# The first two attention steps are set among the layers' last three items

## The chip, the core and the metric

The kernel runs on one core of one Trainium2 chip, in one launch. The metric is the device time of that launch in microseconds (us). TensorE (PE) multiplies, VectorE (DVE), ScalarE (ACT) and GpSimd (POOL) do the rest, SyncE (SP) starts transfers; every engine works through its own list in order, and semaphores tie the lists together.

## The reference

A small language model tower: token embedding, four gated state-space layers, one attention block and one quantised linear map. Cut to what matters:

```
x = embedding[tokens] + pos                     # 32 sequences x 256 tokens x 192
for l in range(4):                              # "the layers"
    h = layernorm(x) * g + b
    u, v = split(h @ Win.T + b_in)
    uc = causal_conv4(u)
    decay = exp(-softplus(uc @ wd.T + bd)); B = uc @ wB.T; C = uc @ wC.T
    y = sum(scan(h = h * decay + uc * B) * C) * sigmoid(v)
    x = x + y @ wo.T + bo
h = layernorm(x)                                # "attention", 12 heads of 16
q, k, v = h @ wq.T, h @ wk.T, h @ wv.T ; rope on q, k
x = x + softmax(q k / 4) v @ wo.T + bo
x = x + int8_matmul(round(layernorm(x) / 0.02), weight) * 0.0002 + bias
```

## The kernel before

All 8192 rows of x (192 wide) stay in on-chip memory. The layers work on **items** of 4 tiles of 128 rows, that is two sequences: 16 items for each of 4 layers, numbered 0 to 63. The attention part works on **sequences**, 0 to 31. Both are software pipelines that are written out by hand: in each step an engine does a stage of one item, another stage of the item before, and so on. `steps` calls `step(at, l, k)` of each engine for the layers, `at(lag)` being the item that entered `lag` steps ago; after the last item has entered there are steps with `l == L` that only drain the pipeline, and k counts them from 0. `steps2` does the same for attention: `step2(at)`, with `at(None)` the number m of the step.

The names that matter here, with item 63 the last one:

- On PE: `z_c` and `b_c` (products for decay, B and C), `transposes`, and `rows`, the output product of an item, which needs the scan's result (`hc_step`, by DVE) for its second half and ends with `o_done`. For attention `turn_x1` transposes the normalised rows, `project_qk(it, t)` (t = 0, 1) and `project_v` multiply them by the weights, `turn_heads(it, g)` (g = 0 to 5) transposes the prepared q and k, and `scores` multiplies them.
- On DVE: `recurrence` (the scan of an item, from inp_h to hc_l), `save_y` and `residual` (x is updated, `x_updated`), and for attention `norm_statistics`, `norm_variances`, `norm_rows`, `save_qk`, `save_v`, `maxima`.
- On POOL: `inverse_deviation2(m)` (seven tiny operations for 1/sqrt), the rotation of q and k, the low parts of q and k (`parts`), and at the seam of the two stages six memsets of constants.
- On ACT: `turned` (a transposed tile to memory), high parts of q and k (`high_parts`), the conversion of the last weights.

Before, the order at the seam is strict: the layers drain in four steps, POOL waits for all items before its memsets, and DVE waits for those, for all items and for ACT's conversion before the first statistics:

```
            pool.wait_ge(x_updated, ITEMS)
            pool.wait_ge(s_w2, W2_ALL)
            nc.gpsimd.memset(parts[:, :, :, :, :, AUG:HS].bitcast(F32), 0.0).then_inc(s_const, 1)
...
            dve.wait_ge(s_const, 7)
            dve.wait_ge(s_w2, W2_ALL)
            dve.wait_ge(x_updated, ITEMS)
```

PSUM has eight banks. The layers use all eight; attention uses the same eight under other names (`B_W` for transposes and projections, `B_S` for scores, `B_ST` for transposed scores, `B_OT` for the outputs).

Of the kernel before, what the change touches and what calls it, by code (L numbers as in the profile page):

```python
# [47 lines left out]
def build(nc, tokens, embedding, pos_enc, w_uv_d, w_z_d, w_o_d, gain_d, vec_d, bout, w_qkv_d, b_qkv_d, w_out_d,  # L48
# [9 lines left out]
    with ExitStack() as ctx:  # L58
# [33 lines left out]
        emb = sb("emb", [P, FIRST, CT * D])  # L92

        layers_memory = ctx.enter_context(ExitStack())
# [10 lines left out]
        w_uv_rest = sa("w_uv_rest", [P, 2, 2, UV_COLS], F32R)  # L105
        w_z = sa("w_z", [P, 2, 2, Z_COLS], F32R)
        w_z_rest = sa("w_z_rest", [P, 2, 2, Z_COLS], F32R)
        w_o = sa("w_o", [P, L, 2, D])
# [6 lines left out]
        xs = sa("xs", [P, CT, 2 * D], F32R)  # L115
        ht = [sa(f"ht_{k}", [P, 2 * S], F32R) for k in range(3)]

# [5 lines left out]
        ucr_h = sa("ucr_h", [P, 2, 2 * S], F32R)  # L123

        ucr_l = sa("ucr_l", [P, 2, 2 * S], F32R)
        ucr_r = sa("ucr_r", [P, 2, 2 * S], F32R)
# [13 lines left out]
        layers_memory.close()  # L140

        qk_rows = sb("qk_rows", [P, 2, 2, 2 * D])
        parts = sb("parts", [P, 2, 2, 2, H, HS], F32R)
        q_t = sb("q_t", [P, 2, H // 2, S], F32R)
        k_t = sb("k_t", [P, 2, H // 2, S], F32R)
        v_rows = sb("v_rows", [P, 2, 2, D])
        v_aug = sb("v_aug", [P, 2, 2, H, 2 * DH])
        probs = sb("probs", [P, 2, 2, 4 * S])
        mx = sb("mx", [P, 2, 2, H])
        mx_t = sb("mx_t", [H, 2, S], F32R)  # L150
        rot = sb("rot", [P, 2, 2 * H, 2, R])
        xn1 = sb("xn1", [P, 2, 2, D])
        h1_t = sb("h1_t", [P, 2 * S])
        o_t = sb("o_t", [P, 3 * S])
        o_sum = sb("o_sum", [P, 2, H])
# [5 lines left out]
        st2 = sb("st2", [P, 4, 6])  # L161
        mv2 = sb("mv2", [P, 4, 2])
        lnt2 = sb("lnt2", [P, 3, 4])
        rstd2 = sb("rstd2", [P, 4])
# [63 lines left out]
        s_const = sem("s_const")  # L228
        mt_placed = [sem(f"mt_placed{k}") for k in range(2)]
# [16 lines left out]
        def steps(eng, step):  # L246
# [16 lines left out]
            for m in range(ITEMS, ITEMS + 4):  # L263
                step(lambda lag, m=m: item(m - lag), L, m - ITEMS)
# [37 lines left out]
        B_S, B_ST, B_OT, B_OT2 = (B_UH, B_VH), (B_UVL, B_ZH), B_BH, B_BL  # L302

        B_W = (B_ZCL, B_CH)
# [59 lines left out]
        def _(pool):  # L364
# [68 lines left out]
            inverse_deviation(item(0))  # L433

            def step(at, l, k):

                for lag, stage in ((-4, index), (-3, gather)):
                    it = at(lag)
                    if it is not None and it[1] == 0 and (l > 0 or k is None or k - lag >= FIRST):
                        stage(it[0], it[2], it[3])  # L440
                inverse_deviation(at(-1))
                bias_rows(at(0))

            steps(pool, step)


            pool.wait_ge(x_updated, ITEMS)
            pool.wait_ge(s_w2, W2_ALL)
            nc.gpsimd.memset(parts[:, :, :, :, :, AUG:HS].bitcast(F32), 0.0).then_inc(s_const, 1)
            nc.gpsimd.memset(v_aug[:, :, :, :, DH:2 * DH], 0.0).then_inc(s_const, 1)  # L450
            pool.wait_ge(s_const, 2)
            for s in range(2):
                nc.gpsimd.memset(parts[:, s, :, 1, :, AUG:AUG + 1].bitcast(F32), 1.0).then_inc(s_const, 1)
                nc.gpsimd.memset(v_aug[:, s, :, :, DH:DH + 1], 1.0).then_inc(s_const, 1)
# [26 lines left out]

            def step2(at):
# [12 lines left out]
                if it is not None:  # L495
                    n, s = it
                    for t in range(2):

                        wait(pool, qk_saved, 2 * n + t + 1)
                        wait(pool, roped, 4 * n + 2 * t)  # L500
                        w = qk_rows[:, s, t].rearrange("p (h i d) -> p h i d", i=2, d=DH // 2)[:, :, :, 0:R]
                        for i in range(2):
                            nc.gpsimd.tensor_tensor(rot[:, 0, :, i, :], w[:, :, 1 - i, :],
                                                    rope[:, 1, t, i, :][:, None, :].broadcast_to([P, 2 * H, R]), ALU.mult)
                        nc.gpsimd.tensor_tensor(rot[:, 1], w,
                                                rope[:, 0, t][:, None, :, :].broadcast_to([P, 2 * H, 2, R]),
                                                ALU.mult).then_inc(roped, 1)
                        wait(pool, roped, 4 * n + 2 * t + 1)
                        nc.gpsimd.tensor_tensor(w, rot[:, 0], rot[:, 1], ALU.add).then_inc(roped, 1)
                    for t in range(2):  # L510

                        wait(pool, hi_ready, 2 * n + t + 1)
# [20 lines left out]
        def _(pe):  # L533
# [138 lines left out]

            means(0)

            def step(at, l, k):
                uv(at(2), prepared(l, k, PREP_CENTRE))
                z_c(at(3))
                transposes(at(1))
# [215 lines left out]
        def _(act):  # L894
# [117 lines left out]
            def step(at, l, k):  # L1012
# [9 lines left out]
                if (to := prepared(l, k, PREP_ROUND)) is not None:  # L1022
                    round_weights(to)
# [521 lines left out]
```

## Time and profile before

| | us |
|---|---|
| median of 3 runs | 1673.48 (1672.98 to 1676.82) |
| the profiled execution, its own time | 1670.43 |
| its span, first to last instruction | 1668.2 |
| PE busy | 1556.8 (93%) |
| DVE busy | 1362.7 (82%) |
| ACT busy | 1241.7 (74%) |
| POOL busy | 741.5 (44%) |

The span is what the trace shows; the 2.2 us between it and the execution's own time lie before the first and after the last instruction. Times of day below are us from the span's start. PE is the busiest engine, but its share is an average over a long stage of layers (to about 988), a seam, and attention (from about 1012 on).

### The profile page before, as it was taken

How to read it: one execution, taken by the hardware profiler on the slowest of the kernel's cores; microseconds unless marked ns; L12 is line 12 of the kernel's file. 1: busy time of each engine (PE TensorE's matmuls, PEld its weight loads, DVE VectorE, ACT ScalarE, POOL GpSimd, SP SyncE). 2: the span in 40 equal slices, each digit the busy share in tenths (PEclk: the TensorE clock that was granted, in tenths of full speed). 3: DMA queues.
4: the chain of work that ended last, by engine and by line, in shares of the span. 5: the costliest groups of instructions: out<-in, count | busy, mean ns of one | idle time of the engine just before them, and what ended most of it. 6: DMA issues, size and time to landing. Idle time of an engine off the chain costs nothing.

```text
span 1668.2 us, 36353 instructions
## 1 busy us (share of the span) xinstructions
PE 1556.8 (93%) x11137; PEld 1223.6 (73%) x11137; DVE 1362.7 (82%) x3414; ACT 1241.7 (74%) x2875; POOL 741.5 (44%) x1354
## 2 busy tenths in 40 slices
PE   3699999999999999999999978999999999999985
PEld 2578788878888788888888864666666666666653
DVE  4699999899999799999999855678888887888864
ACT  2677788788888788888888833777777777777763
POOL 7655633223333233333333115556556555555542
PEclk9789999999999999999999987999999999999997
DMA  7121100000000000000000000000000000000000
GB/s 169 28 56 29 24 6 1 1 33 0 0 1 1 1 1 0 0 1 1 1 0 0 1 0 1 2 7 12 11 10 10 15 10 10 10 10 10 15 12 25
DMA packets 16397, 21.98 MB, mean 13 GB/s; under 512 B 2928, under 2 KB 13808, under 8 KB 16304
## 3 DMA queue, kind: packets, MB, share of 16 engines
q1 hardware_dynamic: 13232, 14.54, 2.7%
q0 software_dynamic: 3072, 6.30, 2.3%
q8 instruction: 47, 0.77, 0.2%
q14 instruction: 46, 0.38, 0.1%
HBM read 14.14 MB, written 6.29 MB: 12 GB/s over the span
## 4 chain that ended last, share of the span: by engine, by line
PE 76%; ACT 9%; DVE 6%; issue 6%; POOL 2%; DMA 1%; DVEq 0%; ACTq 0%; POOLq 0%
PE bank L569 14%; PE bank L560 11%; PE bank L764 5%; PE bank L721 4%; PE bank L650 4%; PE bank L735 4%; PE bank L748 4%; PE bank L580 3%; PE bank L707 3%; PE bank L700 3%; PE bank L710 3%; PE bank L621 3%; PE bank L701 3%; PE bank L657 3%; PE bank L654 2%
## 5 line engine op out<-in xcount | busy, mean ns | idle before, releaser
L1046 ACT ACTIVATE probs<-bank 128x512 f32<-128x512 f32 x384 | 207.1, 592 | 131.3 <-PE bank L748 128.5
L1376 DVE TENSOR_REDUCE mx<-bank 128x2 f32<-128x512 f32 x384 | 246.1, 682 | 22.7 <-PE bank L735 21.5
L430 POOL TENSOR_TENSOR x<-x,bo_row 128x768 f32<-128x768 f32 (+1 forms) x64 | 118.2, 1847 | 196.1 <-DVE ucr_r L1244 196.1
L560 PE MATMUL bank<-ht,w_uv 128*128 128x512 f32 x576 | 171.3, 407 | 16.7 <-ACT sv_l L1005 12.3
L748 PE MATMUL bank<-q_t,k_t 64*128 64x256 f32 x768 | 156.2, 350 | 8.5 <-ACT probs L1046 5.5
L406 POOL TENSOR_TENSOR lnt<-mv,const 128x4 f32<-128x4 f32 x64 | 20.4, 320 | 311.6 <-DVE mv L1209 311.5
L1235 DVE SCALAR_TENSOR_TENSOR uc_h<-u_h,vec,uc_h 128x512 f32<-128x512 f32 x192 | 143.2, 746 | 3.5 <-ACT uc_h L943 3.5
L560 PEld LDWEIGHTS bank<-ht,w_uv 128*128 128x128 f32 x576 | 109.2, 193 | 48.5 <-issue 17.5
L1218 DVE SCALAR_TENSOR_TENSOR xs<-x,rstd,xs 128x192 fp32r<-128x192 f32 x256 | 90.0, 414 | 65.9 <-ACT xs L982 65.9
L735 PE MATMUL bank<-k_t,q_t 64*128 64x256 f32 x768 | 135.9, 316 | 6.1 <-DVE mx L1376 2.6
L748 PEld LDWEIGHTS bank<-q_t,k_t 64*128 64x128 f32 x768 | 102.3, 186 | 39.1 <-issue 20.1
L922 ACT ACTIVATE u_l<-bank,vec 64x256 f32<-64x256 f32 x128 | 60.1, 469 | 85.5 <-PE bank L560 84.7
L560 PE MATMUL bank<-ht,w_uv_rest 128*128 128x512 f32 x384 | 123.0, 402 | 0.0
L514 POOL TENSOR_TENSOR parts<-qk_rows,parts 128x192 fp32r<-128x192 f32 x128 | 77.1, 623 | 95.9 <-ACT parts L1067 95.8
L939 ACT ACTIVATE uc_l<-bank,vec 64x256 f32<-64x256 f32 x128 | 71.9, 562 | 56.8 <-DVE inp_l L1261 55.8
L569 PE MATMUL bank<-ucr_h,w_z 128*128 128x512 f32 x256 | 108.8, 425 | 4.9 <-ACT ht L972 4.9
L721 PE MATMUL bank<-identr,parts 128*128 128x128 f32 x768 | 104.4, 260 | 4.8 <-issue 3.4
L735 PEld LDWEIGHTS bank<-k_t,q_t 64*128 64x128 f32 x768 | 95.6, 188 | 14.5 <-ACT k_t L1057 8.9
L972 ACT ACTIVATE ht<-bank 128x512 fp32r<-128x512 f32 x192 | 100.8, 597 | 4.8 <-PE bank L621 3.3
L764 PE MATMUL bank<-probs,v_aug 128*32 128x256 f32 x1536 | 103.5, 387 | 0.2 <-issue 0.2
L982 ACT ACTIVATE xs<-x,rstd 128x192 fp32r<-128x192 f32 (+1 forms) x256 | 95.6, 444 | 9.7 <-POOL rstd L418 8.1
L569 PE MATMUL bank<-ucr_r,w_z 128*128 128x512 f32 x256 | 102.0, 398 | 0.0
(178 smaller groups left out, 4618.1 us busy)
## 6 DMA issues: line engine op xcount, KB each, us to landing
out_dram<-y_out SPq DMA_DIRECT2D x32, 192.0 KB, 2.0
raw_z<-w_z_dram SPq DMA_DIRECT2D x4, 704.0 KB, 5.3
raw_uv<-w_uv_dram SPq DMA_DIRECT2D x4, 576.0 KB, 3.9
emb<-embedding_dram,idx POOLq DMA_INDIRECT x64, 3.6
q_t<-mx_t SPq DMA_DIRECT2D x64, 6.0 KB
w_o<-w_o_dram SPq DMA_DIRECT2D x1, 768.0 KB, 5.3
bo_row<-bout_dram SPq DMA_DIRECT2D x4, 96.0 KB, 6.0
w_qkv<-w_qkv_dram SPq DMA_DIRECT2D x1, 288.0 KB, 6.6
```

The lines of the kernel that those rows point to most:

```text
L430: nc.gpsimd.tensor_tensor(rows, rows, bo_row[:, l, :][:, None, :].broadcast_to([P, CT, D]), ALU.add).then_inc(x_biased, 1)
L560: last = nc.tensor.matmul(out[:], w, r[:], start=(k == 0), stop=(k == len(passes) - 1))
L569: last = nc.tensor.matmul(out[:], w, r[:, b, :], start=(k == 0), stop=(k == len(passes) - 1))
L721: last = nc.tensor.transpose(B_HEADS[g][:, (2 * o + t) * P:(2 * o + t + 1) * P].bitcast(F32R), parts[:, s, t, o, 2 * g:2 * g + 2, :].rearr ...
L735: last = nc.tensor.matmul(B_S[j][:, t * S:(t + 1) * S], q_t[q, s, g, t * P:(t + 1) * P], k_t[q, s, g, :], start=True, stop=True)
L748: last = nc.tensor.matmul(B_ST[j][:, t * S:(t + 1) * S], k_t[q, s, g, t * P:(t + 1) * P], q_t[q, s, g, :], start=True, stop=True)
L764: last = nc.tensor.matmul(bank[32 * h:32 * h + 32, c:c + S], v_aug[:, s, t, 4 * p + h, :], probs[:, (s + p) % 2, h // 2, (2 * (h % 2) + t) ...
L972: last = act.activation(ht[g][:], B_T[g][:], ACT.Identity)
L982: last = act.activation(xs[:, k, 0:D], x[:, tile_of(c, k)], ACT.Identity, scale=rstd[:, s, k:k + 1])
L1046: last = act.activation(probs[:, (s + g // 2) % 2, g % 2, 2 * j * S:2 * (j + 1) * S], B_ST[j][:], ACT.Exp, scale=float(DH) ** -0.5)
L1235: nc.vector.scalar_tensor_tensor(out=uc, in0=uk, scalar=v(l, part, V_W0 + k), in1=uc, op0=ALU.mult, op1=ALU.add).then_inc(taps, 1)
L1376: last = nc.vector.tensor_reduce(mx[:, s, :, j * H // 2 + g], B_S[j][:].rearrange("p (t k) -> p t k", t=2), AX, ALU.max)
```

## The change

The first two steps of `steps2` (m = 0 and 1: the norms of sequences 0 and 1, and q, k and v of sequence 0) no longer stand behind the layers. Each engine does its part of them inside the layers' drain steps `l == L`, k = 0, 1, 2. There are three such steps now; of the fourth, `rows(63)` on PE and `recurrence(63)`, `save_y(63)`, `residual(63)` on DVE have moved into attention's step m = 2. POOL's memsets wait only until the last product that reads the memory under them is done. So that early steps find free memory and free banks, the attention banks are renamed and the buffers stand in another order; no buffer changes its size.

```diff
-            for m in range(ITEMS, ITEMS + 4):
+            for m in range(ITEMS, ITEMS + 3):
                 step(lambda lag, m=m: item(m - lag), L, m - ITEMS)
...
+        EARLY = 2
...
-            for m in range(LEAD2):
+            for m in range(EARLY, LEAD2):
...
-        B_S, B_ST, B_OT, B_OT2 = (B_UH, B_VH), (B_UVL, B_ZH), B_BH, B_BL
-        B_W = (B_ZCL, B_CH)
+        B_W, B_S, B_ST, B_OT, B_OT2 = (B_VH, B_UVL), (B_BH, B_BL), (B_UH, B_ZH), B_ZCL, B_CH
...
POOL
-            pool.wait_ge(x_updated, ITEMS)
+            def attention_constants():
+                pool.wait_ge(uh_done, ITEMS)
...
+                if l == L and k == 0:
+                    inverse_deviation2(0)
+                    pool.wait_ge(s_w2, W2_ALL)
+                elif l == L and k == 1:
+                    pool.wait_ge(xn1_ready, 1)
+                    add_rows(0, b_out, x1_biased)
+                    inverse_deviation2(1)
+                    attention_constants()
+                elif l == L and k == 2:
+                    rotate(seq(0))
+                    pool.wait_ge(xn1_ready, 2)
+                    add_rows(1, b_out, x1_biased)
...
PE
+            def step(at, l, k):
+                first = l == L and k == 2
+                uv(at(2), prepared(l, k, PREP_CENTRE))
+                z_c(at(3))
+                transposes(at(1))
+                if first:
+                    pe.wait_ge(s_w2, W2_ALL)
+                    pe.wait_ge(sv_ready, ITEMS)
+                    turn_x1(seq(0))
+                rows(at(4))
+                if first:
+                    project_qk(seq(0), 0)
+                b_c(at(3))
+                if first:
+                    project_qk(seq(0), 1)
+                    pe.wait_ge(qk_saved, 1)
+                    project_v(seq(0))
+                    pe.wait_ge(qk_saved, 2)
+                    turn_x1(seq(1))
...
             def step2(at):
+                early = isinstance(at(None), int) and at(None) == EARLY
+                if early:
+                    rows(item(ITEMS - 1))
+                    pe.wait_ge(v_saved, 1)
+                    pe.wait_ge(inp_step, 2 * ITEMS)
...
ACT
+                if l == L and k == 0:
+                    act.wait_ge(s_w2, W2_ALL)
...
+                elif l == L and k == 2:
+                    save_h1(seq(0))
+                    act.wait_ge(s_const, 6)
+                    high_parts(seq(0), 0)
+                    high_parts(seq(0), 1)
...
DVE
+            def norm_early(m):
+                dve.wait_ge(x_updated, ITEMS - NCH + 1)
+                dve.wait_ge(var2_ready, m + 1)
+                norm_statistics(seq(m), None)
+                dve.wait_ge(stats2_done, m + 1)
+                wait(dve, rstd2_ready, m)
+                wait(dve, xn1_ready, m)
+                norm_variances(seq(m), None)
...
                 statistics_there(at(-1))
+                if early and k == 0:
+                    nc.vector.memset(mv2[:], 1.0).then_inc(var2_ready, 1)
+                elif early and k == 1:
+                    norm_rows(0, seq(0), 0, xn1[:, 0], xn1_ready)
+                elif early:
+                    norm_rows(1, seq(1), 0, xn1[:, 1], xn1_ready)
...
                 residual(at(4))
+                if early and k < 2:
+                    norm_early(k)
+                elif early:
+                    dve.wait_ge(s_w2, W2_ALL)
+                    save_qk(seq(0), 0)
+                    save_qk(seq(0), 1)
+                    save_v(seq(0))
...
             def step2(at):
+                early = isinstance(m, int) and m == EARLY
+                if early:
+                    recurrence(item(ITEMS - 1))
+                    dve.wait_ge(x_updated, ITEMS - 1)
...
                 save_qk(at(1), 0)
+                if early:
+                    save_y(item(ITEMS - 1))
+                    residual(item(ITEMS - 1))
...
                 normalise(at(5), 0)
                 maxima(at(2), 1)
```

First place, PE at the seam. Before, from `rows(63)` (L650 to L660) through `turn_x1(0)` (L693, L695), `project_qk(0, 0)` and `(0, 1)` (L700, L701), `project_v(0)` (L707, L710), to the first `turn_heads` (L721), `turn_x1(1)` and the first `scores` (L735):

```order
L650 MATMUL bank<-w_o,sv_h 128x192 x4
L654 MATMUL bank<-ones,hc_h 128x1 x4
L657 MATMUL bank<-w_o,sv_l 128x192 x4
L660 MATMUL bank<-ones,hc_l 128x1 x4
L693 MATMUL bank<-ident,xn 128x128 x2
L695 MATMUL bank<-ident,xn 64x128 x2
...
L707 MATMUL bank<-w_qkv,h_t 128x192 x2
L710 MATMUL bank<-w_qkv,h_t 128x192 x2
L721 MATMUL bank<-identr,parts 128x128 x4
L693 MATMUL bank<-ident,xn 128x128 x2
L695 MATMUL bank<-ident,xn 64x128 x2
L735 MATMUL bank<-k_t,q_t 128x256 x4
```

Of the change, the same functions in new lines: behind the last of `b_c(63)` (L595) come `project_qk(0, 1)` (L711, L712), `project_v(0)` (L718, L721), `turn_x1(1)` (L704, L706), then `rows(63)` (L676 to L686), `turn_heads` (L732) and `scores` (L746):

```order
L595 MATMUL bank<-ucr_l,w_z_rest 128x512
L711 MATMUL bank<-w_qkv,h_t 128x384
L712 MATMUL bank<-w_qkv,h_t 128x384
L718 MATMUL bank<-w_qkv,h_t 128x192 x2
L721 MATMUL bank<-w_qkv,h_t 128x192 x2
L704 MATMUL bank<-ident,xn 128x128 x2
L706 MATMUL bank<-ident,xn 64x128 x2
L676 MATMUL bank<-w_o,sv_h 128x192 x4
...
L686 MATMUL bank<-ones,hc_l 128x1 x4
L732 MATMUL bank<-identr,parts 128x128 x4
L746 MATMUL bank<-k_t,q_t 128x256 x4
```

Everything that stood between `rows(63)` and the first `turn_heads` now stands ahead of `rows(63)`; `turn_x1(1)` has left its place behind the first `turn_heads`. (`turn_x1(0)` stands further up, ahead of `rows(62)`, and `project_qk(0, 0)` between `rows(62)` and `b_c(63)`.)

Second place, DVE. Before, `save_y(62)` and `residual(62)` (L1288, L1299), then `recurrence(63)` (L1258 to L1280), then `save_y(63)` and `residual(63)`:

```order
L1288 COPY ysb<-bank 128x2 x2
L1299 SCALAR_TENSOR_TENSOR x<-bank,ysb,x 128x192 x4
L1258 SCALAR_TENSOR_TENSOR inp_h<-bank,vec,uc_h 128x512
...
L1280 TENSOR_TENSOR hc_l<-cb_l,hs_l 128x256
L1288 COPY ysb<-bank 128x2 x2
L1299 SCALAR_TENSOR_TENSOR x<-bank,ysb,x 128x192 x4
L1343 MEMSET mv 128x8
```

Of the change, from `residual(62)` (L1360) on: `save_qk(0, 0)` and `(0, 1)` (L1416), `save_v(0)` (L1425), then `recurrence(63)` (L1319 to L1341):

```order
L1360 SCALAR_TENSOR_TENSOR x<-bank,ysb,x 128x192 x4
L1416 TENSOR_TENSOR qk_rows<-bank,b_qkv 128x384 x2
L1425 COPY v_rows<-bank 128x384
L1319 SCALAR_TENSOR_TENSOR inp_h<-bank,vec,uc_h 128x512
...
L1341 TENSOR_TENSOR hc_l<-cb_l,hs_l 128x256
L1379 BN_STATS st<-x 128x6 x2
L1406 TENSOR_REDUCE mx<-bank 128x2 x2
L1386 BN_AGGR mv<-st 128x2 x2
L1416 TENSOR_TENSOR qk_rows<-bank,b_qkv 128x384
L1349 COPY ysb<-bank 128x2 x2
L1360 SCALAR_TENSOR_TENSOR x<-bank,ysb,x 128x192 x4
L1406 TENSOR_REDUCE mx<-bank 128x2 x2
```

`recurrence(63)` has moved behind three reads of PE's projections, and `residual(63)` between the first and the second pair of maxima (L1406). Beyond the seam the four engines' lists are the same as before but for bank numbers.

## Rows read from the trace of the kernel before

**Rows 1.** Windows by stage; busy us of each engine, granted clock, DMA share, GB/s.
```profile
980.00:1010.00 30.00, 16.59 (x63) 10.65 (x62) 9.74 (x29) 2.88 (x11) 11.71 (x30) 0.59 0.00 0
...
1100.00:1300.00 200.00, 197.30 (x1761) 133.54 (x1758) 162.42 (x378) 150.77 (x428) 115.12 (x229) 1.00 0.04 11
```

**Rows 2.** Timeline of PE at the layers' end: start, duration, instructions, idle before.
```profile
976.23 0.95 PE L654 MATMUL bank<-ones,hc_h 128*128 128x1 f32 x8
...
978.30 0.50 PE L569 MATMUL bank<-ucr_h,w_z 128*128 128x512 f32 x1
...
981.90 1.46 PE L650 MATMUL bank<-w_o,sv_h 128*128 128x192 f32 x8
984.87 1.20 PE L654 MATMUL bank<-ones,hc_h 128*128 128x1 f32 x8 [1.51 <-DVE hc_l L1280]
987.44 0.85 PE L660 MATMUL bank<-ones,hc_l 64*128 64x1 f32 x8
```

**Rows 3.** The chain that ended last, across the seam: start, us, what.
```profile
990.12 1.38 POOL parts L449
...
999.98 1.62 PE bank L700 x2
1001.60 1.59 PE bank L701 x2
...
1007.08 0.57 DVE qk_rows L1386
...
1012.17 0.72 PE bank L721 x4
```

**Rows 4.** Timeline of DVE, items 62 and 63, and the first norm.
```profile
972.17 0.74 DVE L1258 SCALAR_TENSOR_TENSOR inp_h<-bank,vec,uc_h 128x512 f32<-128x512 f32 x1
...
975.63 0.41 DVE L1280 TENSOR_TENSOR hc_l<-cb_l,hs_l 128x256 f32<-128x256 f32 x1
...
980.94 0.75 DVE L1258 SCALAR_TENSOR_TENSOR inp_h<-bank,vec,uc_h 128x512 f32<-128x512 f32 x1 [0.79 <-PE bank L580]
...
988.34 0.23 DVE L1288 COPY ysb<-bank 128x2 f32<-128x2 f32 x2 [3.52 <-PE bank L660]
...
993.54 0.62 DVE L1349 BATCH_NORM_STATS2 st<-x 128x6 f32<-128x192 f32 x2
994.20 0.25 DVE L1356 BATCH_NORM_AGGREGATE mv<-st 128x2 f32<-128x6 f32 x2
997.25 0.67 DVE L1365 TENSOR_SCALAR xn<-x,mv,rstd 128x192 f32<-128x192 f32 x2 [2.80 <-POOL rstd L480]
```

**Rows 5.** The chain again: the projections later, at the full clock.
```profile
1018.62 0.72 PE bank L700 x2
...
1021.38 0.72 PE bank L707 x4
```

**Rows 6.** Timeline of DVE in step m = 2.
```profile
1017.45 0.56 DVE L1386 TENSOR_TENSOR qk_rows<-bank,b_qkv 128x384 f32<-128x384 f32 x1 [1.34 <-PE bank L701]
1017.92 1.28 DVE L1376 TENSOR_REDUCE mx<-bank 128x2 f32<-128x512 f32 x2
...
1021.89 0.96 DVE L1365 TENSOR_SCALAR xn<-x,mv,rstd 128x192 f32<-128x192 f32 x2
```

**Rows 7.** Timeline of PE: transposes and scores in step m = 2.
```profile
1012.70 0.65 PE L693 MATMUL bank<-ident,xn 128*128 128x128 f32 x2
...
1013.74 0.80 PE L735 MATMUL bank<-k_t,q_t 64*128 64x256 f32 x4
...
1019.72 0.69 PE L735 MATMUL bank<-k_t,q_t 64*128 64x256 f32 x2
```

**Rows 8.** One window of one us, columns as in Rows 1.
```profile
1016.00:1017.00 1.00, 1.00 (x7) 0.37 (x5) 0.11 (x2) 0.00 (x0) 0.73 (x2) 0.82 0.00 0
```

**Rows 9.** Windows of the steps m = 2 and m = 5 of attention.
```profile
1012.17:1027.60 15.43, 12.29 (x68) 8.28 (x68) 8.88 (x17) 6.60 (x22) 9.39 (x21) 0.83 0.00 1
...
1062.62:1081.65 19.03, 17.98 (x163) 12.60 (x161) 12.31 (x26) 13.95 (x40) 10.21 (x22) 1.00 0.01 2
```

More of the change, by code:

```diff
@@ L431, in bias_rows @@
                                         ALU.add).then_inc(x_biased, 1)
[L433 to L444, printed above, removed]
-            pool.wait_ge(x_updated, ITEMS)
[L448 to L454, printed above, removed]
+            def attention_constants():
+                pool.wait_ge(uh_done, ITEMS)
+                nc.gpsimd.memset(parts[:, :, :, :, :, AUG:HS].bitcast(F32), 0.0).then_inc(s_const, 1)
+                nc.gpsimd.memset(v_aug[:, :, :, :, DH:2 * DH], 0.0).then_inc(s_const, 1)
+                pool.wait_ge(s_const, 2)
+                for s in range(2):
+                    nc.gpsimd.memset(parts[:, s, :, 1, :, AUG:AUG + 1].bitcast(F32), 1.0).then_inc(s_const, 1)
+                    nc.gpsimd.memset(v_aug[:, s, :, :, DH:DH + 1], 1.0).then_inc(s_const, 1)
             def add_rows(n, bias, sem_):
@@ new lines, in _ @@
+            inverse_deviation(item(0))
+            def step(at, l, k):
+                for lag, stage in ((-4, index), (-3, gather)):
+                    it = at(lag)
+                    if it is not None and it[1] == 0 and (l > 0 or k is None or k - lag >= FIRST):
+                        stage(it[0], it[2], it[3])
+                inverse_deviation(at(-1))
+                bias_rows(at(0))
+                if l == L and k == 0:
[10 more added lines that the diff above has]
+                    add_rows(1, b_out, x1_biased)
@@ L482, in step2 @@
+            steps(pool, step)
             def step2(at):
@@ L495, in step2 @@
                 if it is not None:
[L496 to L512, printed above, removed]
[L513 to L518 removed]
+                    rotate(it)
                 it = at(0)
@@ L673, in _ @@
             means(0)
[L675 to L678, printed above, removed]
-                rows(at(4))
-                b_c(at(3))
-                if (to := prepared(l, k, PREP_MEANS)) is not None:
-                    wait(pe, sv_ready, at(2)[0] + 1)
-                    means(to)
-            steps(pe, step)
-            pe.wait_ge(s_w2, W2_ALL)
-            pe.wait_ge(s_const, 6)
             def rows_turned(src, dst, idn):
@@ L841, in emptied, with step @@
                     wait(pe, sem_, count * it[0] + add)
-            def step2(at):
+            def step(at, l, k):
+                first = l == L and k == 2
[16 more added lines that the diff above has]
+                    turn_x1(seq(1))
+                if (to := prepared(l, k, PREP_MEANS)) is not None:
+                    wait(pe, sv_ready, at(2)[0] + 1)
+                    means(to)
+            steps(pe, step)
+            def step2(at):
+                early = isinstance(at(None), int) and at(None) == EARLY
[3 more added lines that the diff above has]
+                    pe.wait_ge(inp_step, 2 * ITEMS)
+                elif isinstance(at(None), int) and at(None) == EARLY + 2:
+                    pe.wait_ge(x_updated, ITEMS)
                 for g in range(6):
@@ L876, in step2 @@
                         emptied(at, 8, y_ready, 1, 1)
-                        turn_x1(at(1))
+                        if not early:
+                            turn_x1(at(1))
                     elif g == 1:
@@ L1097, in step2 @@
                         save_o(at(5))
[L1098 to L1099 removed]
+                        if not early:
+                            save_h1(at(1))
                     elif g == 3:
```

166 lines of the change are left out of this document (95 added, 71 removed).

## The prediction, before the result was known

> **What bounds the kernel now.** I read the windows by stage first, to see where PE, the busiest engine, is not busy. In the attention loop it is busy 197.3 of 200 us at full clock [rows 1]; nothing to gain there but work. The seam between layers and attention is another matter: in the 30 us from 980 PE is busy 16.6, at a mean granted clock of 0.59 [rows 1]. So the next views are the timelines of PE and DVE at the layers' end and the chain of work that ended last across the seam. In PE's timeline the last product of the layers, the tail of `rows(63)` (L654 to L660), runs from 984.87 to 987.44 + 0.85 = 988.29, behind a wait of 1.51 for DVE's hc_l, the end of `recurrence(63)` [rows 2]. From there to PE's first `turn_heads` at 1012.17 the chain is a relay of single steps in which each engine waits for the one before: POOL's memset at 990.12, PE's projections from 999.98, DVE's save of them at 1007.08, PE again at 1012.17 [rows 3]. That is 1012.17 - 988.29 = 23.9 us, and the chain passes through every link of it, so what leaves it leaves the time. Behind it attention's steps follow each other at 15.4 us (m = 2) to 19.0 us (m = 5) [rows 9], and all 32 sequences go through them: an earlier first `turn_heads` moves everything behind it.
>
> **The change, part by part.** I carry two times through: when `rows(63)` ends, and when the first `turn_heads` can start.
>
> *Removed.* The 23.9 us above. In their place the first `turn_heads` waits for `rows(63)`, which stands right ahead of it on PE, and for q and k of sequence 0. The steps before are done in the drain.
>
> *Added to the drain, before item 63's B product.* `turn_x1(0)` stands ahead of `rows(62)`. Its four transposes took 1013.74 - 1012.70 = 1.04 at half clock [rows 7]; PE is at full clock here, estimate 0.5. DVE's `norm_early(1)` delays `recurrence(62)`: from 993.54 to 994.20 + 0.25 = 994.45 the same work took 0.91 [rows 4]. hc_l of item 62 then ends at 975.63 + 0.41 + 0.91 = 976.95 instead of 976.04 [rows 4], and the tail of `rows(62)` starts at 977.0 instead of 976.23 [rows 2]: 0.8, which contains the 0.5. Then `project_qk(0, 0)`: two pairs of float32 matmuls over 384 columns. Such a pair cost 1.62 and 1.59 in the slow stretch [rows 3], and the first of them 0.72 at full clock [rows 5]; the other has as many columns, so 1.4 here. B of item 63 is ready 2.2 later, at 980.94 + 2.2 = 983.1 [rows 4].
>
> *The same edit on DVE's list.* `recurrence(63)` stands behind `save_qk(0, 1)` and `save_v(0)`. PE ends `b_c(63)` where it began `rows(63)`, 981.90 [rows 2], plus 2.2 = 984.1; then `project_qk(0, 1)`, 1.4, and `project_v(0)`, two groups of four over 192 columns, 0.72 for the first [rows 5], 1.4 for both: 987.0. The copy of v takes 0.6, as the saves do [rows 3, 6]. So `recurrence(63)` starts at 987.65 and not at 980.94 [rows 4]: 6.7 late, of which 4.5 is this place in the list and 2.2 the work above. What is late next is PE: `turn_x1(1)` and the first half of `rows(63)` are through by 988.9, then PE waits for hc_l until 991.5. The tail took 988.29 - 984.87 = 3.4 in the slow stretch [rows 2] and 978.30 - 976.23 = 2.07 for item 62, at the full clock (`b_c(63)` begins at 978.30 right behind it) [rows 2]. Before, a gap of 1.51 was enough for the granted clock to fall while the tail ran, so with a gap of 2.6 I take the slow price: `rows(63)` ends at 988.29 + 6.7 = 995.0.
>
> *q and k of sequence 0.* `save_qk(0, 1)` is at 985.6. From the same save to the first `turn_heads` it was 1012.17 - 1007.08 = 5.1 [rows 3] (rotation, high parts, low parts), so they are there at 990.7, 4.3 before they are asked for. That slack hides POOL's and ACT's part. POOL's memsets, seven small operations twice and x's bias stand where POOL had been idle; without that cover each us of them beyond 4.3 would count. ACT's conversion and `save_h1` fall into its own waits for PE.
>
> The first `turn_heads` is thus at 995.0 instead of 1012.17: **17.2 gained**.
>
> *Step m = 2 of attention.* DVE now does `save_y(63)` and `residual(63)` there, between `save_qk(1, 0)` and `maxima(0, 1)`. Before, they began at 988.34 [rows 4], and POOL's memset, which waited for their end, at 990.12 [rows 3]; less the hand-over that is 1.7. Queued behind them are the maxima, and PE's next scores wait for those. Before, these maxima ran 1017.92 to 1019.20 [rows 6] and PE's last two scores of the next pair came at 1019.72 [rows 7], 0.5 later. So 1.2 of the 1.7 shows. `turn_x1(1)` and its copy are gone from this step, but the scores behind it waited for ACT's copies anyway; I give it 0.2. **1.0 lost.** PE's wait for `v_saved` and for `inp_step` ends before 992; ACT's new wait for `x_updated` at m = 4 is past by then.
>
> *Edits at nothing:* the bank names and buffer places. The same instructions run, and in the rows above nothing ties a price to a bank or an address. The steps from m = 3 on are the same lists.
>
> Sum: 17.2 - 1.0 = **16.2 us**. The profiled execution took 1670.43, so 1654.2 for it; its sum stands 3.05 below the median of the runs shown, 1673.48, which I take as the base: 1657.3.
>
> **A rule on shared memory ports.** Norm rows of DVE took 0.67 with POOL idle [rows 4] and 0.96 in step m = 2 with POOL at work [rows 6]; the change lays POOL's memsets and `inverse_deviation2(1)` beside `recurrence(62)` and `norm_rows(1)`. The sum above leaves this out, since `norm_rows(1)` has 1.5 us before `save_y(62)` can start, and only a slower `recurrence(62)` reaches PE. The Trainium skill ("GPSIMD Engine Reference", Specifications) says that GpSimd's on-chip memory interfaces are shared with VectorE, with contention for DVE instructions in a two-port mode or with two inputs in that memory; the norm rows agree with it, and by it the scans, which read two such inputs, would slow as well.
>
> **The rivals.**
> 1. *The clock stays low through step m = 2.* After the gap before the tail PE has shorter ones (behind the first `turn_heads`, where `turn_x1(1)` no longer fills the wait for ACT's copies). Before, the clock came back at 1016 to 1017 [rows 8], 4 us after the first `turn_heads`. If it does not come back within the step, `project_qk(1, 0)` pays some 0.7 more, `project_qk(1, 1)` and `project_v(1)` 3.2 - 1.4 = 1.8 each, with a little for transposes: 4.5 at most. Gain 11.7, time 1661.8. Speaks for it that the clock was low for most of the 30 us of the seam [rows 1]; against it that the densest four us brought it back.
> 2. *The clock does not fall before the tail.* The wait could be shorter, or PE's dense work ahead of it could carry it. Tail 1.35 less, and the first 4 us of m = 2 save 3.2 - 1.4 = 1.8 at `project_qk(1, 0)`; with `residual(63)` hidden, 1.0 more. Gain 20.4, time 1653.1. Against it: a gap of 1.51 was enough before [rows 2].
> 3. *POOL slows the recurrence.* If `recurrence(62)` takes 0.96 / 0.67 = 1.43 times its 3.9 us, all behind it is 1.7 late. Gain 14.5, time 1659.0. Against it: most of its instructions read PSUM for one input.
> 4. *Slower: the renamed banks cost the loop.* Every step from m = 2 on uses the new banks. If DVE's maxima or ACT's exponentials (12 instructions of each in a step) became slower by some 0.06 us each, a step would be 0.7 longer, and over 30 steps 21, so 16.2 - 21 = 5 slower, 1678. That is the point from which it decides: 0.7 on 19.0 [rows 9]. Nothing in the trace shows a price that hangs on the bank's number.
> 5. *No change: the drain grows by as much as it saves.* Each hand-over in drain step k = 2 would have to be 5 us longer than summed (PE waits for `save_qk(0, 0)`, DVE for PE, PE for hc_l: three of them). 1670 to 1674. Against it: all three engines wait for PE there, and PE's part is priced above.
>
> **How the numbers follow.** Forecast 0.63, rival 1 0.14, rival 2 0.11, rival 3 0.06, rival 4 0.03, rival 5 0.03. The range takes in the first four: from rival 2's 1653.1 to rival 1's 1661.8, with a bit of the median's own scatter above, 1653 to 1662.5. A measurement of this kernel tells a difference of about 0.3% (5 us) from none. Faster by more than that: forecast and rivals 1 to 3, 0.94; within it 0.03; slower 0.03.
>
> **What would show it.** In the profile of the changed kernel: `recurrence(63)` starts right behind the copy of v, 6 to 7 us later than 980.94; PE waits 2 to 3 us for hc_l inside `rows(63)`, and its tail is slow; the first `turn_heads` follows `rows(63)` at once, at about 995, 16 to 18 earlier than before; no wait of POOL, ACT or DVE over 10 us at the seam; the second pair of maxima in m = 2 stands behind the residual; the step at m = 5 is still 19.0 us. Wrong would be: a `turn_heads` that waits for the low parts (then POOL's drain work is the bound), a clock at half through 1005, or a loop step of another length.

## The result, and the profile of the changed kernel

The changed kernel takes 1657.51 us (median of 4 runs, 1652.08 to 1660.74), the kernel before 1673.61: a ratio of 0.9909, 95% interval 0.9893 to 0.9926. The forecast was 1657.3. A second set of six runs gave 1657.11 and 0.9907 (0.9888 to 0.9926). The median is as forecast; the profile shows that it came about in another way, with two terms that I had left out and that pull opposite ways.

The profiled execution took 1659.81 us, its span is 1657.9, 10.3 less than before. What follows accounts for these 10.3 us between two executions; the medians lie 16.1 apart. First the seam, in the timeline of PE:

```profile
969.17 0.38 PE L704 MATMUL bank<-ident,xn 128*128 128x128 f32 x2
969.39 0.38 PE L706 MATMUL bank<-ident,xn 128*64 128x128 f32 x2
969.61 1.47 PE L676 MATMUL bank<-w_o,sv_h 128*128 128x192 f32 x8
971.15 1.05 PE L680 MATMUL bank<-ones,hc_h 128*128 128x1 f32 x8
...
973.33 0.91 PE L711 MATMUL bank<-w_qkv,h_t 128*128 128x384 f32 x2
...
981.88 0.44 PE L704 MATMUL bank<-ident,xn 128*128 128x128 f32 x2
...
982.38 1.47 PE L676 MATMUL bank<-w_o,sv_h 128*128 128x192 f32 x8
987.44 1.05 PE L680 MATMUL bank<-ones,hc_h 128*128 128x1 f32 x8 [3.60 <-DVE hc_l L1341]
988.43 1.49 PE L683 MATMUL bank<-w_o,sv_l 64*128 64x192 f32 x8
989.70 0.86 PE L686 MATMUL bank<-ones,hc_l 64*128 64x1 f32 x8
990.49 0.75 PE L732 MATMUL bank<-identr,parts 128*128 128x128 f32 x4
992.08 0.80 PE L746 MATMUL bank<-k_t,q_t 64*128 64x256 f32 x4 [0.84 <-ACT k_t L1082]
```

Before, the last z product ended and `rows(62)` began at 974.94:

```profile
974.94 1.46 PE L650 MATMUL bank<-w_o,sv_h 128*128 128x192 f32 x8
```

`turn_x1(0)` stands at 969.17 ahead of `rows(62)`, all projections of sequence 0 lie between there and 982, `rows(63)` has one wait inside it, 3.60 us for hc_l, its tail is slow for the most part (987.44 to 990.49), and the first `turn_heads` (L732) follows at once. Against [rows 2, 3], where the same stretch went from 974.94 to 1012.17, that is 37.2 us, it now takes 990.49 - 969.17 = 21.3. So 15.9 us are gained here.

DVE and POOL at the same place, from their timelines:

```profile
971.02 2.12 DVE L1395 TENSOR_SCALAR xn<-x,mv,rstd 128x192 f32<-128x192 f32 x2
...
982.47 0.74 DVE L1319 SCALAR_TENSOR_TENSOR inp_h<-bank,vec,uc_h 128x512 f32<-128x512 f32 x1
...
983.51 1.87 DVE L1328 TENSOR_TENSOR_SCAN hs_h<-dc_h,inp_h 128x256 f32<-128x256 f32 x2
985.31 1.00 DVE L1332 TENSOR_TENSOR_SCAN hs_l<-dc_l,inp_l 128x256 f32<-128x256 f32 x1
...
986.88 0.51 DVE L1341 TENSOR_TENSOR hc_l<-cb_l,hs_l 128x256 f32<-128x256 f32 x1
```

```profile
970.61 1.38 POOL L447 MEMSET parts<- 128x1536 f32 x1
...
982.76 3.01 POOL L499 TENSOR_TENSOR parts<-qk_rows,parts 128x192 fp32r<-128x192 f32 x4
985.73 1.37 POOL L456 TENSOR_TENSOR x<-x,b_out 128x384 f32<-128x384 f32 x1
```

`recurrence(63)` starts right behind the copy of v, as forecast, and takes 982.47 to 987.39 = 4.9 us instead of 3.9, while POOL works beside it, which itself is slower.

Second, the steps of attention behind it, and the stretch at the low clock (windows, columns as in [rows 1]):

```profile
990.49:1010.51 20.02, 16.82 (x67) 11.07 (x65) 10.48 (x23) 5.96 (x20) 8.91 (x20) 0.50 0.00 1
1010.51:1031.07 20.56, 18.93 (x77) 12.21 (x75) 10.68 (x21) 7.62 (x24) 9.99 (x22) 0.50 0.00 1
1031.07:1052.10 21.03, 19.22 (x129) 11.85 (x127) 10.79 (x21) 13.74 (x37) 9.95 (x22) 0.71 0.01 2
1052.10:1071.00 18.90, 17.86 (x162) 12.53 (x160) 12.30 (x26) 13.83 (x40) 10.20 (x22) 1.00 0.01 2
```

```profile
988.00:1044.00 56.00, 50.52 (x221) 32.55 (x220) 26.27 (x55) 20.16 (x59) 23.96 (x53) 0.51 0.00 1
```

Step m = 2 takes 20.0 us and not 15.4 as in [rows 9], m = 3 20.6 and not 16.2, m = 4 21.0 and not 18.8; only m = 5 is back at 18.9. In the 56 us from 988 PE is busy 50.5 and the granted clock is 0.51. From the first `turn_heads` to m = 5 it is 61.6 us, before 50.4: 11.2 lost, where I had 1.0.

Third, what I did not look at: the layers. The chain of work in the middle of the third layer, of before and of the change, where it holds PE alone:

```profile
641.46 3.49 PE bank L560 x15
644.95 2.34 PE bank L569 x10
```

```profile
639.46 3.40 PE bank L586 x15
642.86 2.27 PE bank L595 x10
```

The first row is the u and v product of an item, the second the z product. Both got shorter, 0.16 us an item together, though neither their code nor their order changed. At the seam this execution is 974.94 - 969.17 = 5.8 us ahead. The steps in the middle of the layers gather some 6.6 us in about 45 items; the start of the kernel and the hand-overs between layers take 0.8 back here, and they differ between executions: `rows(62)` begins at 971.7 to 977.9 in the three profiles with the buffers in their old order, and, where `turn_x1(0)` is moved too, at 968.2 to 974.3 in the seven with the new one. So the gain of an item is steady and the 5.8 is of these two executions. The account of the spans is then -5.8 - 15.9 + 11.2 and 0.2 in the rest: -10.3.

### The profile page after: what moved, and what is told of

Its sections match the earlier page's. It is cut to its first block, busy times and chain, and to the rows that moved or that the text cites. A ratio compares the mean times of both kernels' runs of the same rounds, so it can differ in the third digit from the quotient of the medians.

```text
span 1657.9 us, 36360 instructions
## 1 busy us (share of the span) xinstructions
PE 1555.3 (94%) x11137; PEld 1229.3 (74%) x11137; DVE 1365.5 (82%) x3414; ACT 1238.9 (75%) x2875; POOL 747.5 (45%) x1354
## 4 chain that ended last, share of the span: by engine, by line
PE 62%; ACT 14%; DVE 12%; issue 9%; POOL 1%; DMA 1%; DVEq 1%; ACTq 0%; POOLq 0%
PE bank L595 9%; PE bank L586 7%; PE bank L775 5%; PE bank L732 4%; PE bank L746 4%; PE bank L718 4%; PE bank L759 4%; PE bank L711 3%; PE bank L721 3%; PE bank L712 3%; PE bank L676 3%; ACT xs L1028 2%; DVE x L1360 2%; ACT ht L1018 2%; PE bank L606 2%
## 5 line engine op out<-in xcount | busy, mean ns | idle before, releaser
L1406 DVE TENSOR_REDUCE mx<-bank 128x2 f32<-128x512 f32 x384 | 246.1, 682 | 26.6 <-PE bank L746 25.0
L417 POOL TENSOR_TENSOR lnt<-mv,const 128x4 f32<-128x4 f32 x64 | 20.5, 321 | 311.9 <-DVE mv L1270 311.8
L746 PE MATMUL bank<-k_t,q_t 64*128 64x256 f32 x768 | 141.2, 325 | 6.2 <-ACT k_t L1082 3.1
L759 PEld LDWEIGHTS bank<-q_t,k_t 64*128 64x128 f32 x768 | 103.0, 188 | 39.7 <-issue 21.3
L595 PE MATMUL bank<-ucr_h,w_z 128*128 128x512 f32 x256 | 107.5, 420 | 5.6 <-ACT ht L1018 5.4
L746 PEld LDWEIGHTS bank<-k_t,q_t 64*128 64x128 f32 x768 | 99.1, 194 | 16.0 <-ACT k_t L1082 9.1
L732 PE MATMUL bank<-identr,parts 128*128 128x128 f32 x768 | 105.9, 263 | 2.2 <-issue 2.1
L1081 ACT ACTIVATE q_t<-bank 128x256 fp32r<-128x256 f32 x192 | 73.5, 383 | 45.0 <-PE bank L732 44.9
L647 PE MATMUL bank<-identr,xs 128*128 128x128 f32 x768 | 76.2, 247 | 29.1 <-DVE xs L1279 18.3
```

What stands on the lines that cost most here:

```text
L595: last = nc.tensor.matmul(out[:], w, r[:, b, :], start=(k == 0), stop=(k == len(passes) - 1))
L732: last = nc.tensor.transpose(B_HEADS[g][:, (2 * o + t) * P:(2 * o + t + 1) * P].bitcast(F32R), parts[:, s, t, o, 2 * g:2 * g + 2, :].rearr ...
L746: last = nc.tensor.matmul(B_S[j][:, t * S:(t + 1) * S], q_t[q, s, g, t * P:(t + 1) * P], k_t[q, s, g, :], start=True, stop=True)
L759: last = nc.tensor.matmul(B_ST[j][:, t * S:(t + 1) * S], k_t[q, s, g, t * P:(t + 1) * P], q_t[q, s, g, :], start=True, stop=True)
L1406: last = nc.vector.tensor_reduce(mx[:, s, :, j * H // 2 + g], B_S[j][:].rearrange("p (t k) -> p t k", t=2), AX, ALU.max)
```

## The experiments

Each kernel was timed against the kernel before on the same chip; "mean clock" is the granted clock over a whole run.

**The changed kernel again.**

> The changed kernel itself, more executions and a second profile. Clock theory: after the gap of 3.6 us inside rows(63) PE runs at 1.2 GHz for a stretch whose length differs between executions (54.6 us in the first profile, of it steps m = 2 and 3 at 20.0 us each instead of 15.4 and 16.2), so the time scatters between some 1652 and 1661 and goes against the mean granted clock of the execution, about 0.3 to 0.4 us per us at the low clock; the median stays near 1657. Rival, order theory: steps m = 2 and 3 are long because of residual(63) on VectorE and the renamed banks; then they are 19 to 20 us in every profile, whatever the clock, and the times agree within 3 us.

Six runs: 1652.35, 1652.74 and 1655.34 at mean clocks of 0.970 or 0.971, 1658.88, 1660.54 and 1661.75 at 0.963 or 0.964. The scatter goes with the clock. Its profile has the low stretch again, 54.6 us from 989 on, and steps of 20.0 and 20.6 us for m = 2 and 3. The order theory allowed no such scatter, but it is not refuted by this run alone. (The clock theory says that the steps are long because TensorE runs at the low clock, the order theory that they are long because of what was moved into them.)

**recurrence(63) earlier on DVE.**

```diff
                     save_qk(seq(0), 0)
+                    recurrence(item(ITEMS - 1))
                     save_qk(seq(0), 1)
                     save_v(seq(0))
...
                 if early:
-                    recurrence(item(ITEMS - 1))
                     dve.wait_ge(x_updated, ITEMS - 1)
```

> Of the changed kernel, recurrence(63) stands on VectorE right behind save_qk(0, 0), ahead of save_qk(0, 1) and save_v(0). Step of the prediction under test: of the 6.7 us by which recurrence(63) was to be late, 4.5 are this place in the list. If so, the scan starts when B is ready, the wait of TensorE for hc_l inside rows(63) goes (3.6 us in the profile), q and k of sequence 0 come 1 to 1.5 us later, and the first turn_heads starts about 3.4 us earlier: 1654 by the order alone. Clock theory adds: with no gap the clock stays at 2.4 GHz into step m = 2, 3 to 8 us more, 1647 to 1651, and less scatter. Rival: the low parts by GpSimd become what turn_heads waits for, nothing gained, 1657.

1652.45 us (5 runs), ratio 0.9875 (0.9859 to 0.9891); the profile is of the slowest of the five, 1656.71. The wait inside `rows(63)` is gone, in PE's timeline:

```profile
973.42 0.38 PE L704 MATMUL bank<-ident,xn 128*128 128x128 f32 x2
...
986.80 1.47 PE L676 MATMUL bank<-w_o,sv_h 128*128 128x192 f32 x8
988.10 0.95 PE L680 MATMUL bank<-ones,hc_h 128*128 128x1 f32 x8
...
990.71 0.51 PE L732 MATMUL bank<-identr,parts 128*128 128x128 f32 x4 [0.47 <-POOL parts L499]
992.06 0.50 PE L746 MATMUL bank<-k_t,q_t 64*128 64x256 f32 x4 [0.84 <-ACT k_t L1082]
```

From `turn_x1(0)` at 973.42 to the first `turn_heads` it is 17.3 us instead of 21.3: 4.0 less, so the place in DVE's list was worth what the prediction gave it. The other half, a clock that stays up and 1647 to 1651, failed: the clock fell at 992, behind gaps of 0.47 and 0.84, and stayed low for 44 us.

**The wait inside rows(63) filled.**

```diff
+                if isinstance(n, int) and n == ITEMS - 1:
+                    pe.wait_ge(decay_ready, ITEMS)
+                    filler(5)
                 wait(pe, hc_step, 2 * (n + 1))
...
+            def filler(count):
+                for _ in range(count):
+                    nc.tensor.matmul(B_ZCL[:, 0:2 * D], w_qkv[:, 0, 0:P], w_qkv[:, 0, 0:2 * D], start=True, stop=True)
```

> Of the changed kernel, TensorE does five float32 matmuls of 384 columns (0.72 us each, 3.6 us) into a bank that nothing uses, between the first and the second half of rows(63), where it waited 3.6 us. Their results are not used. Nothing else changes, so the order theory gives 1657, or up to 0.5 more. Clock theory: no gap, the clock does not fall at 988; steps m = 2 and 3 shorter by up to 4 us each unless the 0.84 us gap behind the first turn_heads brings it down anyway: 1649 to 1654.

1654.7 us (4 runs, 1651.03 to 1656.46), ratio 0.9902 (0.9887 to 0.9917): 2.4 to 2.8 under the changed kernel's medians, but the intervals overlap, and 0.7 above the 1649 to 1654 of the clock theory. The profile, of the fastest of the four runs, tells the theories apart. Step m = 2:

```profile
994.35:1009.34 14.99, 10.53 (x67) 7.10 (x65) 10.38 (x23) 5.96 (x20) 8.58 (x20) 0.93 0.00 1
```

15.0 us instead of 20.0, with the same instructions in the same order from the first `turn_heads` on. m = 3 took 15.9, and m = 5 began 49.1 behind the first `turn_heads` instead of 61.6. So the long steps are the clock's, and the order theory falls; two profiles with the old order, below, say the same. That the filling keeps the clock up is less sure: two of the four runs took 1656.2 and 1656.5 at mean clocks of 0.967 and 0.966 and were not profiled. At full clock the price of `residual(63)` also shows, as PE's wait for the second maxima:

```profile
1002.11 0.51 PE L749 MATMUL bank<-k_t,q_t 64*128 64x256 f32 x4 [1.10 <-DVE mx L1413]
```

1.1 us, where the prediction had 1.2. (`filler` itself began at 988.41 and ended 0.38 before hc_l came.)

**Names and places alone.** The kernel before, with `B_W`, `B_S`, `B_ST`, `B_OT`, `B_OT2` and the order of buffers taken from the change.

> The kernel before, with the new bank names and the new order of buffers and nothing else. The prediction priced both at nothing: 1673 to 1674, within 0.2% of before, and a step m = 5 of 19.0 us. Rival (renamed banks or places cost the attention loop): 0.1 us a step or more, 1676 and up.

1673.08 us (12 runs), ratio 0.9996 (0.9975 to 1.0017). As forecast, for the wrong reason. Four of the runs took 1662.62 to 1665.63 at mean clocks of 0.965 to 0.969, eight took 1671.58 to 1678.11 at 0.954 to 0.960; of the 17 runs of before beside them 15 were at 0.965 or above. The profile is of a run of the first kind: items 36 to 47 of the layers take 13.69 us each, before 13.85, and `rows(62)` starts at 969.1 instead of 974.9, while the attention steps are those of before (m = 2, 3 and 5 take 15.4, 16.2 and 19.0). So the new places make the layers some 6 us shorter in this execution, and the median of all twelve shows nothing of it: in most runs something at a lower clock takes it back. No run of the second kind was profiled.

**Bank names alone.** Only the five names.

> The kernel before with the new bank names alone, every buffer where it was. In all five profiles with the new order of buffers an item of the layers takes 13.69 us, in the one profile of before 13.85 (items 36 to 47). Theory (the places of the buffers make TensorE's products in the layers faster): here an item takes 13.85 again, and the time is that of before at the same mean clock. Rival (it differs from execution to execution, or the bank names do it): 13.69.

1672.74 us (10 runs), ratio 1.0006 (0.9984 to 1.0027), and 13.85 us an item: the bank names do nothing, the order of the buffers does.

**xs and ht moved alone; ucr moved alone.**

```diff
+        xs = sa("xs", [P, CT, 2 * D], F32R)
+        ht = [sa(f"ht_{k}", [P, 2 * S], F32R) for k in range(3)]
         w_z = sa("w_z", [P, 2, 2, Z_COLS], F32R)
```

> The kernel before with xs and ht placed ahead of w_z, as in the change, and nothing else. If the places of moving operand or weights make the difference, either the uv product of an item (15 matmuls, 3.49 us before, 3.40 after) or the z product (10 matmuls, 2.34 and 2.27) is the shorter one here, the item 13.76 to 13.80; if it needs both moves, 13.85.

> The kernel before with ucr_h, ucr_l and ucr_r placed ahead of w_o, as in the change, and nothing else. If the place of ucr makes it, the z product alone gets shorter (2.27) and an item takes 13.78; if not, 13.85.

One run each, so that only the profile is used; the chain in the third layer, first with xs and ht moved, then with ucr moved:

```profile
653.72 3.44 PE bank L560 x15
657.15 2.33 PE bank L569 x10
```

```profile
654.54 3.50 PE bank L560 x15
658.04 2.27 PE bank L569 x10
```

ucr moved: the z product alone goes from 2.34 to 2.27, all of its gain. xs and ht moved: the u and v product goes to 3.44, half of its gain. An item takes 13.77 with the one and 13.80 with the other. Moving one buffer also shifts those that it passes, so neither run moves one operand alone. And with xs and ht moved, the u and v product reads its two operands, ht and w_uv, from the very places of the change and yet has only half of the gain; what gives the other half was not found. The B and C products read the same ucr buffers and did not change: 1.17 for five matmuls before, 1.16 after. Each 512-column matmul went from 0.233 to 0.227 us in the products that changed.

**Constants early alone.** Names and places, and of the moves only POOL's memsets (at `l == L`, k = 1) and ACT's conversion (k = 0).

> The kernel with the new names and places, and of the moves only this: GpSimd's six memsets and ScalarE's conversion of weights stand in the drain; VectorE's first norm waits for the last item alone. No step of attention is moved. By the prediction's relay the first turn_heads comes 3.4 us nearer to the end of rows(63) (20.5 instead of 23.9 us), so 3 us less than names and places alone at the same clock.

1667.39 us (10 runs, 1664.58 to 1674.29), ratio 0.9976 (0.9959 to 0.9994), 5.7 under names and places alone where 3 were forecast; the ratios' intervals (0.9975 to 1.0017 there) overlap. In the chain of the profile DVE's first norm no longer waits for POOL and ACT:

```profile
981.00 1.07 DVE x L1310 x3
982.32 0.63 DVE st L1361 x2
982.97 0.26 DVE mv L1368 x2
...
1001.08 0.72 PE bank L731 x4
```

PE's last L670 there ended at 980.3, and the first `turn_heads` is 20.8 later: 3.1 less than 23.9, forecast 3.4. The rest of the difference of the medians was not explained.

In this profile the clock was low for 75 us from 978 on, and so it was, from 985 on, in the run with ucr moved alone. Both have the old order of attention's steps and none of the change's new hand-overs. Their windows:

```profile
978.00:1054.00 76.00, 61.42 (x239) 37.47 (x238) 31.45 (x73) 23.69 (x71) 36.18 (x81) 0.51 0.00 1
```

```profile
985.00:1061.00 76.00, 58.30 (x222) 35.09 (x222) 31.46 (x73) 24.51 (x74) 38.53 (x87) 0.51 0.00 1
```

Steps m = 2 and 3 took 20.0 and 20.5 us in the one, 20.0 and 20.6 in the other, as in the changed kernel. So these lengths are the low clock's price in either order, and a low clock that lasts through m = 2 and 3 is not the new order's alone: two of the seven profiles with the old order have it.

**The seam of before, filled.** Thirteen fillers in PE's wait of 9.8 us.

```diff
             pe.wait_ge(s_w2, W2_ALL)
+            pe.wait_ge(sv_ready, ITEMS)
+            for _ in range(13):
+                nc.tensor.matmul(B_VH[:, 0:2 * D], w_qkv[:, 0, 0:P], w_qkv[:, 0, 0:2 * D], start=True, stop=True)
             pe.wait_ge(s_const, 6)
```

> The kernel before; TensorE, which idles 9.8 us between rows(63) and the first transposes of attention, does 13 float32 matmuls of 384 columns (0.72 us each) there, into a bank that nothing uses. Their results are not used; the order is as before. Clock theory: the clock stays at 2.4 GHz over the seam, so the three projections of sequence 0 take 1.4 instead of 3.2 us each and the first steps are shorter: 6 to 9 us less, 1663 to 1666. Order theory: nothing, 1671 to 1672.

1674.42 us (10 runs), ratio 1.0028 (1.0013 to 1.0043): slower. A miss. The profile is of the fastest of the ten, 1670.49; it, too, needs longer from the end of `rows(63)` to step m = 5, 77.6 us where before needed 74.3. The timeline shows where:

```profile
996.98 0.88 PE L703 MATMUL bank<-w_qkv,h_t 128*128 128x384 f32 x2 [0.83 <-ACT h_t L1040]
...
999.36 1.64 PE L703 MATMUL bank<-w_qkv,h_t 128*128 128x384 f32 x2 [0.65 <-DVE qk_rows L1389]
```

The first projection ran at full clock, then the waits of the relay (0.83, 0.65) stood ahead of its fall at 999, later than in before and for longer: it came back at 1034, behind step m = 2, which took 20.0 us. Here, to fill one gap ahead of others only moved the fall.

**Six fillers, with recurrence(63) early.** One pair of 0.72 us (as in `filler(1)`) behind `rows(63)`, behind the first `turn_heads`, and behind the fourth and fifth `turn_heads` of m = 2 and 3.

> The changed kernel with recurrence(63) behind save_qk(0, 0) (as in the run before) and one filling matmul of 0.72 us, whose result is not used, in six places of TensorE's order in which it waits anyway: behind rows(63), behind the first turn_heads, and behind the fourth and fifth turn_heads of steps m = 2 and 3. Clock theory: the low clock after 990 is gone or short (steps m = 2 and 3 at 15 to 16 us, not 20), time 1644 to 1648 with little scatter. Rival (fillers cost what they bring, the scatter comes from elsewhere): 1651 to 1654, as without them.

1650.13 us (6 runs, 1645.8 to 1653.59), ratio 0.9874 (0.9852 to 0.9897), mean clocks 0.972 to 0.977. The clock was low for three pieces of 3.4 us only, but step m = 2 took 17.1 us where it had 15.0 with none in it. Three of the fillers stand in it, 2.2 us, and one of the low pieces; how the 2.1 divide between them was not tried. Above the forecast of 1644 to 1648.

**The residual ahead of the maxima.**

```diff
+                if early:
+                    save_y(item(ITEMS - 1))
+                    residual(item(ITEMS - 1))
                 maxima(at(2), 0)
...
                 if early:
-                    save_y(item(ITEMS - 1))
-                    residual(item(ITEMS - 1))
                     dve.wait_ge(s_const, 6)
```

> The changed kernel with recurrence(63) behind save_qk(0, 0), and save_y(63) and residual(63) ahead of the first maxima of step m = 2 instead of behind save_qk(1, 0). VectorE waits 5.1 us there for the first scores, so they cost nothing; behind save_qk(1, 0) TensorE waited 1.1 us for the maxima behind them at full clock, and nothing at the low clock. So 0 to 1.1 us less than with recurrence(63) moved alone at the same mean clock: 1651 to 1652.5. Rival (residual is hidden anyway): 1652.5.

With `recurrence(63)` early: 1651.1 us (6 runs), ratio 0.9874 (0.9851 to 0.9898). 1.3 under the run without it, within what these runs scatter; not settled by the time. DVE's timeline shows that the residual is covered there (a wait of 0.49 for the scores is left behind it):

```profile
985.09 1.39 DVE L1360 SCALAR_TENSOR_TENSOR x<-bank,ysb,x 128x192 f32<-128x192 f32 x4
986.98 1.29 DVE L1406 TENSOR_REDUCE mx<-bank 128x2 f32<-128x512 f32 x2 [0.49 <-PE bank L746]
```

**Both, and two fillers.** `recurrence(63)` and residual early, `filler(1)` behind `rows(63)` and behind the first `turn_heads`.

> The same, and two filling matmuls pairs of 0.72 us whose results are not used, behind rows(63) and behind the first turn_heads. The two gaps of 0.5 and 0.8 us go, so that the clock falls later or not at all around 992; against the run with six fillers, whose steps m = 2 and 3 paid for four of them: 1647 to 1650, mean granted clock 0.970 to 0.975. Rival (only many fillers hold the clock): as without them, 1651.

1644.53 us (6 runs, 1641.14 to 1650.14), ratio 0.9833 (0.9807 to 0.9858), mean clocks 0.970 to 0.981: the fastest version, 13 us under the changed kernel, and 2.5 below the forecast's lower bound. Step m = 2:

```profile
987.80:1002.00 14.20, 11.07 (x68) 7.43 (x66) 10.36 (x21) 5.96 (x20) 9.35 (x21) 0.93 0.01 1
```

PE waits for the maxima no longer in its first half, and the clock stays up until 1000. Over the seam and the first steps the clock was low for 14 us or less in each of the three profiles with fillers in the new order (this one, the six fillers, and the filled wait), and for 31 to 55 us in the four without.

## Why the number was right, and what was wrong

*The 23.9 us relay goes, and moves everything behind it.* Right. The forecast for the first `turn_heads` was 17.2 earlier; in the profile it is 15.9, measured from the end of the last z product. Of the 1.3 that are missing, 0.6 are that `recurrence(63)` starts 13.3 us behind that point instead of the 12.7 that I had (before 6.0): a projection costs 1.6 to 1.7 at full clock when nothing runs beside it (973.33 to about 975.0), and I took 1.4. Another 1.0 is the slower recurrence; the tail, nearly 0.4 shorter than I had, works the other way.

*recurrence(63) waits for two saves, 4.5 of its delay.* Right, and shown: with the scan first, 4.0 came back.

*POOL beside DVE: left out of the sum.* This step failed, in a place that I had not named. The rival had `recurrence(62)` slowed; it was `recurrence(63)`, by 1.0 us, next to POOL's low parts and its add of x's bias, and `norm_rows(1)`, 2.12 instead of 0.67 next to the memset, which was covered as forecast. The rule of the Trainium skill ("GPSIMD Engine Reference", Specifications), contention for VectorE's instructions with two inputs in on-chip memory, agrees: the scans have two. `inp_h` and `hc_h`, which read PSUM for one input, kept their 0.74 and 0.72 beside the same work of POOL. With the recurrence moved ahead, to where POOL was idle, the first two scans took 1.26 again; with the wait filled and the overlap as in the change, 1.87 again. `recurrence(62)`, beside POOL's seven tiny operations only, was not slowed.

*The tail runs at the low clock.* Right for its larger part: 987.44 to 990.49 is 3.1, forecast 3.4; its first eight products still took 1.05 and not 1.20. So rival 2, a clock that stays up, did not come.

*residual(63) costs 1.2 in m = 2.* Right at full clock (1.1 us). At the low clock it hides behind PE: part of a term that holds in one of two states.

*The low clock ends within step m = 2.* This step failed, and was rival 1 at 0.14; a clock at half through 1005 was also my own sign of being wrong, and it came. The rival had a bound of 4.5, since I looked at one step only; the clock stayed low through m = 2 and m = 3 and part of m = 4, 4.6, 4.4 and 2.2 us, 10 us more than the forecast had. That the steps are long by the clock is shown: filled, the same list took 15.0, and the old list at the low clock took 20.0. My argument against the rival, that four dense microseconds had brought the clock back before, was one execution of before; in the run with ucr moved alone the same list did not bring it back for 75 us.

*"Edits at nothing: the bank names and buffer places."* The names are nothing, as measured. The places are not, in the profiles: 0.16 us an item, near 6 us at the seam. In the medians of names and places alone nothing is left of it. This is the step that failed without any rival to hold it. I had reasoned from the attention buffers and not asked what else moves in the layers: xs, ht, ucr, w_z.

*Rivals 4 and 5.* Neither came. Attention's step m = 5 takes 18.9 to 19.0 us in every profile, before and after.

So 1.3 less gained and 10 more lost than forecast on one side, 5.8 on the other: they do not cancel. For this execution the forecast of its own time was 1654.2, and it took 1659.8. The base of the median stood 3 us above before's profiled execution, the changed kernel's profiled execution lies 2.3 above its median, and its runs scatter over 9 us with the clock; these took up the difference. The agreement within 0.2 us is luck; the range was right to be ten us wide.

**What stays open.** What decides how long the low clock lasts was not found: stretches of 20 to 75 us were seen with PE busy 76 to 90% in them, and one of 31 us, in before, with PE busy 57%. How much of the low clock's length belongs to the change and how much to the execution is open with it. Nor was it found why names and places alone so often run at a low mean clock (8 of 12), or what in the order of the buffers makes a matmul's stream faster; a finer search by addresses was not made.

## What to carry to other kernels

When two stages of a pipeline are laid into each other, look at what the new hand-overs do to TensorE's clock, not only at their own length: here the steps behind the seam took 11 us more at the low clock than before, and two moves on VectorE with two well-placed fillers gave 13 us, about half of it by the fillers. In these runs a filler paid where no other gap followed at once, and did not where one did. Before putting a long low stretch down to the new order, see how often the old order has one: one profile of each does not tell. A change in the order of buffers can change the time of instructions that nobody edited: measure it alone, and compare one period of the steady loop far from the edit.

## What the runs showed of the hardware

- TensorE can stay at 1.2 GHz for a long time while it is busy most of the time: 50.5 of 56 us in the changed kernel, 61 and 58 of 76 us with the constants early alone and with ucr moved alone. Gaps of 0.47 and 0.84 us, with 0.5 us of work between them, stood ahead of one fall.
- With the same code, the run times went with the mean granted clock: the kernel before ran from 1666.11 (0.972) to 1682.58 (0.957) in 29 runs. Wholly at the low clock step m = 2 took 20.0 us in either order of work; in the new order, with a mean granted clock of 0.93, it took 14.2 to 15.0.
- The order of buffers in on-chip memory changed a 512-column matmul from 0.233 to 0.227 us in two of the four products of an item, and not in the others, which read some of the same buffers at another moment. The places of a product's own operands did not settle it: one product had half of the gain with both at their new places.
- GpSimd and VectorE slow each other: two norm rows took 2.12 instead of 0.67 us next to a memset, three scans 2.9 instead of 1.9, GpSimd's four subtractions 3.01 instead of 2.41.
